# New instruction lists for the first five tiles of a gated cross-attention and ternary feed-forward kernel

## The reference

```python
q = rms_norm(linear(layernorm(x), q_w, q_b), norm_q_w)     # 16 heads of 32
k = rms_norm(linear(context, k_img_w, k_img_b), norm_k_img_w)
v = linear(context, v_img_w, v_img_b)
x = x + tanh(g_xattn) * linear(softmax(q k^T / sqrt(32)) v, o_w, o_b)
w1, w2 = ternary(W_fc), ternary(W_proj)   # groups of 64: q*scale, q in {-1,0,1}, scale = mean|w|
h = relu(layernorm(x) w1)**2              # 2048 hidden channels
x = x + tanh(g_ffn) * (rms_norm(h) w2)
```

## Time and profile before

| | us |
|---|---|
| median of 3 runs | 1002.77 (1001.32 to 1004.7) |
| profiled execution | 1004.31 |
| its span, first to last instruction | 1002.5 |
| PE busy in the span | 928.4 (93%) |
| ACT busy | 717.6 (72%) |
| DVE busy | 689.4 (69%) |
| POOL busy | 565.7 (56%) |
| mean granted clock of PE | 0.973 |

### The profile page before, as it was taken

The page is one execution under the profiler, slowest core; times in us unless marked ns, Lnnn a source line. Parts: engine busy times, 40 slices in busy tenths (PEclk is TensorE's granted clock), DMA queues, the critical chain, the costliest instruction groups (busy, mean ns, idle before and its releaser), DMA issues.

```text
span 1002.5 us, 26078 instructions
## 1 busy us (share of the span) xinstructions
PE 928.4 (93%) x9941; PEld 570.9 (57%) x10043; DVE 689.4 (69%) x1360; ACT 717.6 (72%) x1235; POOL 565.7 (56%) x616
## 2 busy tenths in 40 slices
PE   3676687899999999999999999999999999999998
PEld 1343344566656566666656656666665666666664
DVE  7988987876767676777677676767777676766400
ACT  2877766677777777777777777778777777776673
POOL 1223323755666566765657565766656665766484
PEclk9887887999999999999999999999999999999999
DMA  8635333333233444343323344433342344322100
GB/s 303 168 97 147 96 86 63 64 73 77 68 72 75 86 85 75 77 80 74 80 64 73 77 85 85 75 77 84 67 79 69 72 78 86 65 54 54 43 22 32
DMA packets 184588, 82.43 MB, mean 82 GB/s; under 512 B 170000, under 2 KB 170000, under 8 KB 182928
## 3 DMA queue, kind: packets, MB, share of 16 engines
q1 hardware_dynamic: 184464, 80.77, 35.9%
HBM read 30.67 MB, written 8.39 MB: 39 GB/s over the span
## 4 chain that ended last, share of the span: by engine, by line
PE 82%; issue 6%; DVE 4%; ACT 4%; POOL 2%; DMA 1%; SPq 0%; DVEq 0%; POOLq 0%; ACTq 0%
PE mix_ps L440 11%; PE up_pair L426 10%; PE up_pair L427 10%; PE mix_ps L439 8%; PE score_ps L395 7%; PE score_ps L397 7%; PE score_ps L396 7%; PE tr_a L395 3%; PE tr_a L396 3%; PE tr_a L397 3%; PE score_ps L510 2%; PE score_ps L487 2%; PE mix_ps L577 2%; DMA big<-in_wq_t 1%; PE tr_a L440 1%
## 5 line engine op out<-in xcount | busy, mean ns | idle before, releaser
L426 PE MATMUL up_pair<-ft,w 128*128 128x256 f16 x960 | 217.1, 275 | 0.6 <-ACT h_sb L798 0.6
L427 PE MATMUL up_pair<-ft,w 128*128 128x256 f16 x960 | 217.1, 275 | 0.0
L1635 POOL TENSOR_TENSOR k_weighted<-k_raw,qk_norm 128x512 f32<-128x512 f32 x32 | 41.8, 1308 | 254.9 <-DVE k_raw L1164 253.3
L440 PE MATMUL mix_ps<-w,big 128*128 128x512 bf16 x464 | 176.1, 380 | 10.0 <-issue 8.6
L1649 POOL TENSOR_TENSOR big<-h_sb,big 128x512 f16<-128x512 f32 x128 | 155.2, 1212 | 15.6 <-ACT h_sb L807 11.2
L1659 POOL TENSOR_TENSOR hh_sum<-hh_sum,hh_sb 128x512 f32<-128x512 f32 x112 | 154.5, 1380 | 3.1 <-ACT hh_sb L820 3.1
L439 PE MATMUL mix_ps<-w,big 128*128 128x512 bf16 x382 | 145.1, 380 | 0.0
L869 ACT ACTIVATE score_ps<-score_ps,log_p,exp_scale 128x512 f32<-128x512 f32 x128 | 95.6, 747 | 58.8 <-PE score_ps L513 58.8
L1076 DVE TENSOR_TENSOR p_lo<-score_ps,p_hi 128x512 f16<-128x512 f32 x128 | 88.1, 689 | 47.6 <-ACT p_hi L751 47.0
L798 ACT ACTIVATE h_sb<-up_pair,relu_scale 128x512 f32<-128x512 f32 x120 | 81.2, 677 | 35.2 <-PE up_pair L427 34.5
L426 PEld LDWEIGHTS up_pair<-ft,w 128*128 128x128 bf16 x960 | 94.5, 98 | 18.4 <-ACT h_sb L798 1.0
(11 more groups left out here) (223 smaller groups left out, 2325.9 us busy)
## 6 DMA issues: line engine op xcount, KB each, us to landing
x_sb<-in_x SPq DMA_DIRECT2D x32, 256.0 KB, 3.0
ctx_sb<-in_ctx_t SPq DMA_DIRECT2D x32, 256.0 KB, 2.7
out<-out_sb SPq DMA_DIRECT2D x32, 256.0 KB, 2.0
big<-in_w_fc_t SPq DMA_DIRECT2D x4, 1024.0 KB, 5.2
big<-in_w_proj_t SPq DMA_DIRECT2D x4, 1024.0 KB, 5.0
big<-in_wq_t SPq DMA_DIRECT2D x1, 1024.0 KB, 7.8
big<-in_wk_t SPq DMA_DIRECT2D x1, 1024.0 KB, 9.8
big<-in_wv_t SPq DMA_DIRECT2D x1, 1024.0 KB, 10.3
```

What stands on the lines that cost most here:

```text
L426: nc.tensor.matmul(dst[:, half], w, ft[i][:, c, :], start=(c == 0), stop=False)
L427: last = nc.tensor.matmul(dst[:, half], w, ft[i][:, C + c, :], start=False, stop=(c == C - 1))
L440: last = nc.tensor.matmul(dst[:, :], ht_lo[i][:, row], w2[:, m, :], start=False, stop=(m == M - 1))
```

## The change

Slots 0 to 4 get new lists on all engines; slots 5 to 31 keep theirs.

- **Context a slot ahead.** ACT sums the magnitudes of a context row (`context_total`, Abs with an accumulated sum, into `ctx_sum`) for tile t+3 at the end of slot t; PE spreads it right behind the transposed scores (`early_context`); `context_top` and `context_scale` of tile t+2 stand ahead of the first `probs_lo` on DVE, and the context's high and low parts of tile t+2 at the end of slot t instead of the start of slot t+1. `context_scale` is three instructions instead of four: k's and o's factors are one pair `unscale[t % 4]`.
- **O behind V.** `project_out(t-1)` stands behind `next_values(t)` instead of ahead of `next_keys(t)`; `x1_out` and `x1_stats` move behind `v_lo_of` on DVE; on POOL `x1_norm` stands ahead of `x_norm`, and `rows_plus_constant` (`xb`) behind it. The low parts of x1 of tiles 0 to 2 move one slot on.
- **v's low part early.** `v_lo_of` stands right behind `q_lo`, with one ternary product between them.
- **Sums.** The largest magnitudes of the weights of q and v become sums of magnitudes by ACT (`weight_sum(0)`, `weight_sum(2)`). The low part of the O weights moves from ahead of the first `probs_lo` of slot 0 to behind `q_out`.
- **Ternary.** The halves 28 to 31 are copied by ACT (`raw_half`) and clipped by DVE as pieces 14 and 15.
- **Fillers.** `warm` is 4, with 2 more in slot 1, ahead of the transposed scores of slots 1 and 2 (10, with 4 more in slot 1), 5 and 2 in slots 3 and 4 (12 and 4); two times 4 stand behind the last two ternary pairs of slots 1 and 2, and 6 at the end of slot 0.
- **SP** issues x's and the attention's transposes of a tile at the head of the next slot.

```diff
             def early_slot(t):                          # tensor
                 scores(t)
                 ternary_pair(p)
-                warm(10)
+                warm(4)
                 tops_t(t)
                 if t == 1:
-                    warm(4)
+                    warm(2)
                 scores_t(t)
+                early_context(t)
                 ternary_pair(p + 1)
-                project_out(t - 1)
                 next_keys(t)
                 next_queries(t)
                 values(t)
                 next_values(t)
-                next_context(t)
+                project_out(t - 1)
                 ternary_pair(p + 2)
+                warm(4)
                 ternary_pair(p + 3)
+                warm(4)
...
+            def context_total(t, par):                  # scalar
+                act.wait_ge(ctx_in[par], 16 * (t // 2 + 1))
+                act.wait_ge(ctx_spread, t)
+                act.wait_ge(qss_ready, max(1, t - 1))
+                if t == 2:
+                    act.wait_ge(kss_ready, 1)
+                nc.scalar.activation(square_out[:, :], ctx_sb[par][:, :], ACT.Abs, accum_out=ctx_sum[:, :]).then_inc(ctx_part_ready, 1)
...
             def first_slot():                           # vector
                 tops_t(0)
                 context_lo(1, 1)
-                weight_lo(3)
+                context_top(2)
+                context_scale(2)
                 probs_lo(0, 0)
...
                 q_out(1)
+                weight_lo(3)
+                k_lo(1)
                 attention(0, 0)
                 attention(0, 1)
...
+            def early_slot(t):                          # gpsimd, slots 0 to 4
+                s = t - 1
+                if s > 2:
+                    hidden_lo(0, 2, 3)
+                    hidden_sum(0, 2, 3)
+                k_weight(t + 1)
+                k_rms_of(t + 1)
+                if s >= 2:
+                    hidden_lo(0, s, 0)
+                q_norm(t + 1)
+                if s >= 2:
+                    hidden_sum(0, s, 0)
+                    hidden_lo(0, s, 1)
+                    hidden_sum(0, s, 1)
+                if s >= 0:
+                    x1_norm(s, s)
+                x_norm(t + 2, (t + 2) % 4)
+                if t == 0:
+                    pool.wait_ge(setup_dve, 1)
+                rows_plus_constant(t, t % J)
+                if s >= 2:
+                    hidden_lo(0, s, 2)
+                    hidden_sum(0, s, 2)
...
+            weight_sum(0)                               # scalar, setup
+            x_hi_first()
             for s in range(3):
+                if s == 2:
+                    weight_sum(2)
                 weight_hi(s)
```

More of the change, by code:

```diff
@@ new lines, in early_slot, with third_slot @@
+                context_total(t + 3, (t + 3) % 2)
+                if t == 1:
+                    ternary_sign(7)
+                    ternary_abs(8)
+                else:
+                    normed_hi(1)
+                    ternary(11)
+                    ternary_abs(12)
+            def third_slot():
+                top_pairs(3)
+                tops(3)
+                ternary_sign(12)
+                softmax(3)
+                key_squares(4)
+                act.wait_ge(ffn_consts, 1)
+                relu(0, 2, 0, up_ps)
+                halves(0, 2, 0)
+                k_hi(4)
+                squares(0, 2, 0)
+                query_squares(4)
+                ternary_abs(13)
+                q_hi(4)
+                relu(0, 2, 1, up_ps)
+                attention_hi(3)
+                halves(0, 2, 1)
+                v_hi_of(4)
+                context_hi(5, 1)
+                squares(0, 2, 1)
+                ternary_sign(13)
+                relu(0, 2, 2, up_ps)
+                x_hi(5)
+                halves(0, 2, 2)
+                ternary_abs(14)
+                relu(0, 2, 3, up_ps)
+                squares(0, 2, 2)
+                halves(0, 2, 3)
+                context_total(6, 0)
+                normed_hi(2)
+                squares(0, 2, 3)
@@ new lines, in fourth_slot @@
+            def fourth_slot():
+                raw_half(2 * NU - 4)
+                top_pairs(4)
+                tops(4)
+                ternary_sign(14)
+                softmax(4)
+                raw_half(2 * NU - 3)
+                key_squares(5)
+                relu(0, 3, 0, up_ps)
+                halves(0, 3, 0)
+                k_hi(5)
+                squares(0, 3, 0)
+                query_squares(5)
+                ternary_abs(15)
+                q_hi(5)
+                relu(0, 3, 1, up_ps)
+                attention_hi(4)
+                halves(0, 3, 1)
+                v_hi_of(5)
+                context_hi(6, 0)
+                raw_half(2 * NU - 2)
+                squares(0, 3, 1)
+                ternary_sign(15)
+                relu(0, 3, 2, up_ps)
+                x_hi(6)
+                halves(0, 3, 2)
+                raw_half(2 * NU - 1)
+                relu(0, 3, 3, up_ps)
+                squares(0, 3, 2)
+                normed_hi(3)
+                halves(0, 3, 3)
+                squares(0, 3, 3)
```

451 lines of the change are left out of this document (243 added, 208 removed).

## The result

The changed kernel takes **1023.55 us** (median of 4 runs, 1022.93 to 1025.21); the kernel before, on the same chip, 1002.96 us (median of 4, 1001.32 to 1004.7). The ratio is 1.0208, 95% interval 1.0186 to 1.0229: 20.6 us slower. The forecast was 1004.7 with a range up to 1009.5. It was wrong by 19 us, and none of its rivals reaches the result either.

A forecast was written before the change was run, and what follows sets the result against it. TensorE bounds slots from 5 on; in slots 0 to 2 DVE is fullest, with ACT and PE in the loop. 3.05 us won at full clock, 5.0 lost to the clock: net 1.95 lost, 1004.7 us, range 993 to 1009.5.

The forecast's parts named there:

- Clock at 0.5 at T2: Sign: granted clock 0.5 at slot 2's transposed-score start and during the first K matmuls of slots 1 to 3.
- Next maxima: Sign on DVE: the next slot's score maxima not before 24.5 us after the slot's transposed scores start.
- xn behind x1n in slots 3 and 4: Sign on POOL: xn waits for x1n in slots 3 and 4, delaying ACT's x_hi.
- The clock's term of 5.0: Slots 1 to 5: fewer fillers leave PE at the lower clock, 5.0 us lost, bounds 0 and 10.
- T1: Start of slot 1's transposed scores on PE: forecast 69.3 instead of 70.02, 0.7 earlier, bounds 0 to 1.7.
- v's low part: Sign on DVE: v_lo done near T+15 to T+17, T being the slot's transposed-score start.
- so both loops close where they closed: Slots 1 and 2: next maxima at T+24.6 (was T+24.8), tops' copy at T+27.1 (was T+27.3).
- Rival 3: POOL's order bounds: slot 3 loses 1.0, slot 4 loses 3.2; 1008.5 us, chance 0.25.
- Slot 3: Step forecast at 36.71 us against 36.46 before: 0.75 won at full clock, 1.0 lost to the clock.
- Slot 4: 1.2 lost: Slot 4 at full clock: x_hi at T+23.8 and DVE's tail delay slot 5's maxima; bounds 0.6 and 3 lost.
- 1.35 and 1.45 won at full clock: Slots 1 and 2: fewer warm matmuls holding the tops' transpose, giving 28.4 and 30.7 against 29.76 and 32.16.
- Rival 1: Slots 0 to 4: 9.9 us taken off DVE shortens the slots one for one; 993 us, chance 0.15.

The follow-up runs named there:

- experiment 1: Changed kernel with POOL making xn of slot t+2 ahead of x1n in slots 0 to 4: 1016.94 us, ratio to before 1.0137.
- the kernel with all four edits: Changed kernel with xn ahead of x1n, old filler counts, slot 0's x1 low part early, pair 15's products and slot 3's x1 low part behind slot 5's maxima: 1007.05 us.
- the kernel before with the new setup: Kernel before with only the changed setup: q and v weight sums by ScalarE instead of VectorE's maxima, O weights' low part left early: 1001.59 us, ratio 0.9983.
- xb 1.9: The kernel with all four edits, plus POOL's addition xb ahead of the two normalizations in slots 1 and 2: 1005.11 us, ratio 1.0010.
- experiment 4: Changed kernel with ternary pair 15's last two products and slot 3's x1 low part moved behind slot 5's score maxima: 1024.24 us, ratio 1.0207.
- experiment 3: Changed kernel with the low part of slot 0's x1 rows right behind v's low part in slot 2: 1022.21 us, ratio 1.0181.

## Why the prediction was wrong

**What held.** First scores at 37.23 (37.7 foretold). Clock at 0.5 at T2 and in K's matmuls of slots 1 and 2 (not in slot 3, where they took 2.77). Next maxima at T + 28.9 in slot 1, not before T + 24.5. xn behind x1n in slots 3 and 4. Slot 5 at 28.03, though my sum had charged it 0.7 more. The clock's term of 5.0 measured 6.3, within its bounds, but its parts were off and made up for each other: the full fillers give slots 1 to 4 back 3.0, 1.5, 0.0 and 2.2, where I had 1.0, 1.6, 1.0 and 0.7. K took 4.81, 5.30 and 4.65 in slots 1, 2 and 4, 1.9 to 2.5 over 2.75, and I had taken half or less of 2.6.

What didn't hold: T1 at 70.13 was foretold at 69.3 and lies just outside its bounds, since slot 0 gave back 1.9. v's low part was done at T + 18.6 and T + 20.2 in slots 1 and 2 (88.00 and 122.68, and 0.69), not at T + 15 to 17; VectorE could take K's results only at T + 9.0 and T + 9.5, not T + 6.05, 2.1 and 2.5 of it by K's own matmuls at the lower level.

**The step that failed first: slots 1 and 2, "so both loops close where they closed".** That is off by 3.6 in slot 1, most of it the clock, and by 6.9 in slot 2. ScalarE's high part of x was to begin at T + 21.1; it began at T + 24.7 and T + 31.3. For xn I counted the statistics alone. The order of x1n ahead of xn I charged to slots 3 and 4 only, and I never asked what x1n itself waits for. The diff moved the low part of slot 0's x1 a slot on and behind a round of ternary products, and x1n waits for it: 5.1 us from the statistics (125.3) to 130.35. Rival 3 had the right engine, but as a matter of statistics that end late. It put 3.75 on it; POOL's order is worth 6.6, and the low part 1.3. A wait that the text of the diff doesn't touch becomes a new one when its releaser moves.

**Slot 3: right by luck.** I had 36.71, and it took 37.84. POOL's order costs 3.1 there (34.75 without it, and the high part of x at T + 29.0 instead of T + 25.7), more than either my sum or rival 3 had; the lists without it would have won 1.7, and the clock that I charged with 1.0 was hardly there (K's twelve in 2.77).

**Slot 4: 1.2 lost, bounds up to 3, measured 9.0.** Two terms were too small. x_hi came at T + 26.8 and not T + 23.8, for the most part because K's twelve matmuls took 1.9 more. And the tail: I took one stall of 0.6 from the earlier trace rows, and there were three in a row (1.75, 1.52, 1.75), beside POOL's additions back to back. POOL's order is not the reason for them: with xn ahead (experiment 1) the same three take 1.76, 1.52 and 1.75. Moving them away is worth nothing alone, and 2.0 on top of the others. By the medians slot 4 and the rest can't be told apart further.

**"1.35 and 1.45 won at full clock".** This rested on the shorter filler, and that was a saving I counted apart from the clock it buys. In the kernel before the two cancel: the few fillers gave slot 1 30.57 (0.8 more) and slot 2 31.39 (0.8 less), 0.6 by the medians, no change within the interval. With the full fillers, POOL's order and the low part mended, slots 1 and 2 of the new lists take 30.24 and 33.40, no less than the 29.76 and 32.16 of before.

**VectorE's relief.** Rival 1 counted 9.9 us off VectorE, 5.4 of it after T0. From T0 to T5 its busy time is 132.17 us before and 131.85 after (21.57 + 26.45 + 28.37 + 28.94 + 26.84; 20.10 + 26.59 + 27.20 + 29.91 + 28.05): what was taken off came back as longer instructions. The products `w<-w,abs_w`, 16 in both, took 11.0 before and 13.6 after, the clips 4.5 (10 of them) and 9.0 (12). Where rows are shown above, the long ones stand beside POOL's additions; I have not matched the others one by one. The kernel with all four edits has 131.95.

**The books.** From 1023.55: clock 6.3, POOL's order 6.6, the low part 1.3, the tail 2.0, xb 1.9. That is 18.1 and would end at 1005.4; measured is 1005.1, where the kernel before with the new setup is at 1001.6. Of the five the clock and POOL's order are clear of the noise each by itself; the low part, the tail and xb are not, or barely. About 3.5 us remain that the new lists cost with these five mended. In the traces of the kernel with all four and of the new setup alone they are 1.4 in slot 0, 0.5 in slot 1, 2.0 in slot 2, 1.3 in slot 4 and 1.6 in slot 5, against 2.6 won in slot 3 (33.97 against 36.60), 4.2 in all, before xb's 1.9; T0 comes 1.4 later in the first of the two, which is no more than T0 differs between executions. What makes each of them I can say for slot 5 (PE's wait for the moved product and the clock behind it) and in part for slots 0 and 2; the rest stays open.

## What to carry to other kernels

For each instruction that a change moves later, list all that wait for it on other engines, also where the code of the wait is untouched. A filler and the work behind it are one term: what a shorter filler saves, the work that then runs at the lower clock can cost, if anybody waits for it. Work taken off a full engine counts only if what it stands beside stays the same; look for the pairs that exclude each other before you book the relief.

## What the runs showed of the hardware

- PE can be busy and stay at the lower level: 8.65 of 9.36 us busy at a granted clock of 0.50, from T2 to the end of K's projection, the scores' matmuls on 32 rows first. I had taken at most half of K's matmuls at that level, and all twelve ran there.
- A clip of VectorE with one input (bf16, 128x1024) took 1.48 us in the changed kernel (at 95.25) and 1.49 in the kernel with all four edits, instead of 0.42, beside POOL's addition xb; that is a stall as long as those with two inputs had. I had booked it for these alone.
- Where in a slot the clock rises differs between executions of the same code: K's twelve matmuls of slot 1 took 4.81 us in the trace of the changed kernel and 4.74 in experiment 4's, but 2.77 in those of experiments 1 and 3, and all four kernels are the same up to there on PE.
